# Layer 0's softmax denominators: VectorE adds all four key blocks, TensorE takes two steps a batch in place of four, and all engines get a new order

## The reference

```python
for L in range(4):
    h = relu(layernorm(x))
    x = x + layer[L](h, adj)

# layer 0: 8 heads of 32, q = k = v = LN(h) * gamma1 + beta1
scores = qkv @ qkv.T / sqrt(32);  attn = softmax(where(adj > 0, scores, -inf))
y = h + attn @ qkv;   out = y + gelu(LN(y) @ W1 + b1) @ W2 + b2
# layers 1 and 2: 4 heads of 64, logits = leaky_relu(src_i + dst_j), masked softmax over j, attn @ (h W)
# layer 3: 4 heads of 64, q, k, v projections, masked softmax (diagonal always kept), relu(out @ Wo + bo)
```

## Time and profile before

| | |
|---|---|
| time, median of 3 runs | 4239.26 us (4238.15 to 4240.6) |
| the profiled execution | 4241.92 us, span 4240.1 us |
| TensorE busy | 4042.6 us, 95% |
| VectorE busy | 3223.4 us, 76% |
| ScalarE busy | 2166.5 us, 51% |
| granted TensorE clock, mean | 0.988 |

### The profile page before, as it was taken

The page is one execution under the profiler, slowest core; times in us unless marked ns, Lnnn a source line. Parts: engine busy times, 40 slices in busy tenths (PEclk is TensorE's granted clock), DMA queues, the critical chain, the costliest instruction groups (busy, mean ns, idle before and its releaser), DMA issues.

```text
span 4240.1 us, 58963 instructions
## 1 busy us (share of the span) xinstructions
PE 4042.6 (95%) x22884; PEld 1929.7 (46%) x22884; DVE 3223.4 (76%) x6473; ACT 2166.5 (51%) x3361; POOL 408.3 (10%) x469
## 2 busy tenths in 40 slices
PE   5799999999999999999999999999999999999997
PEld 1344444444444444444444444444444444444443
DVE  5677778877778877777877777877778877788854
ACT  3454555544555554555544555544555544555532
POOL 0001011101011101110100110100110100110100
PEclk9999999999999999999999999999999999999998
DMA  3111111111111111111111111112111111211000
GB/s 99 29 42 50 56 37 49 34 53 51 56 36 51 31 53 52 56 36 51 31 52 54 56 35 51 31 51 56 56 32 54 31 51 56 56 31 46 21 31 31
DMA packets 212311, 193.90 MB, mean 46 GB/s; under 512 B 144448, under 2 KB 179008, under 8 KB 203584
## 3 DMA queue, kind: packets, MB, share of 16 engines
q1 hardware_dynamic: 212032, 190.12, 15.3%
HBM read 138.95 MB, written 17.56 MB: 37 GB/s over the span
## 4 chain that ended last, share of the span: by engine, by line
PE 90%; DVE 5%; ACT 4%; DMA 1%; issue 1%; SPq 0%; POOL 0%; POOLq 0%; ACTq 0%; DVEq 0%
PE O L477 12%; PE M L425 11%; PE M L438 10%; PE S L358 6%; PE S L524 6%; PE O L371 6%; PE M L491 6%; PE O L540 6%; PE M L449 6%; PE O L481 5%; PE M L502 3%; PE M L416 3%; PE M L582 3%; PE O L382 2%; ACT PP L625 2%; PE M L398 2%
## 5 line engine op out<-in xcount | busy, mean ns | idle before, releaser
L1014 DVE SCALAR_TENSOR_TENSOR PG<-g,tcg,mT 128x512 f32<-128x512 f32 x1024 | 691.2, 742 | 33.1 <-PE O L481 21.4
L625 ACT ACTIVATE PP<-S,reach 128x1024 f32<-128x1024 f32 x512 | 542.6, 1111 | 318.8 <-PE O L371 114.5
L906 DVE TENSOR_TENSOR PP<-PP,mT 128x1024 f32<-128x1024 f32 x512 | 597.3, 1218 | 16.5 <-ACT PP L625 16.0
L477 PE MATMUL O<-PG,V 128*32 128x512 f32 x4096 | 550.9, 602 | 18.5 <-DVE PG L1014 17.0
L425 PE MATMUL M<-hT,W 128*128 128x512 f32 x1024 | 460.6, 603 | 3.1 <-ACT hT L660 2.8
L438 PE MATMUL M<-W,H 128*128 128x256 f32 x2048 | 459.7, 378 | 0.0
L438 PEld LDWEIGHTS M<-W,H 128*128 128x128 f32 x2048 | 377.3, 189 | 71.7 <-issue 10.6
L1126 POOL TENSOR_SCALAR ve<-mv 128x4 f32<-128x4 f32 x192 | 97.8, 509 | 3197.4 <-DVE mv L864 3197.4
L358 PE MATMUL S<-hT 32*128 32x512 f32 x2048 | 301.3, 658 | 30.8 <-ACT PP L625 29.4
L739 ACT ACTIVATE PP<-S,sh 128x1024 f32<-128x1024 f32 x256 | 272.1, 1118 | 87.5 <-DVE Q L916 49.0
L603 ACT ACTIVATE V<-z,nb,rs 128x256 f32<-128x256 f32 x128 | 76.6, 602 | 467.4 <-DVE nb L896 467.4
(11 more groups left out here) (136 smaller groups left out, 5608.5 us busy)
## 6 DMA issues: line engine op xcount, KB each, us to landing
g<-t_rows SPq DMA_DIRECT2D x64, 1024.0 KB, 4.7
adj<-adj_in SPq DMA_DIRECT2D x32, 1024.0 KB, 5.5
x<-x_in SPq DMA_DIRECT2D x32, 512.0 KB, 4.0
z<-t_rows SPq DMA_DIRECT2D x64, 256.0 KB, 4.0
out<-x SPq DMA_DIRECT2D x32, 512.0 KB, 2.9
W<-w_in SPq DMA_DIRECT2D x1, 3072.0 KB, 13.0
mT<-z SPq DMA_TRANSPOSE x128, 2.5
m<-V SPq DMA_TRANSPOSE x128, 2.5
```

Of the source, the lines that this page charges most:

```text
L477: e.matmul(k.O[0][r:r + 32, :], s.V[:, jt, 64 * hh + 32 * v:64 * hh + 32 * v + 32], p[:, u, :], start=(jt == 0), stop=(jt == NT - 1))
L625: e.activation(p[:, 2 * pair:2 * pair + 2, :], k.S[:, 2 * pair:2 * pair + 2, :], ACT.Exp, bias=k.reach[:, 7:8], scale=SC0).then_inc(k.e0.s ...
L906: e.tensor_tensor(p[:, 2 * pair:2 * pair + 2, :], p[:, 2 * pair:2 * pair + 2, :], s.mT[:, jt:jt + 1, :].to_broadcast([128, 2, N]), ALU.mul ...
L1014: e.scalar_tensor_tensor(out=p[:, u, :], in0=s.T[hh], scalar=s.tcg[:, 1, hh, jt:jt + 1], in1=s.mT[:, jt, :], op0=ALU.max, op1=ALU.mult).th ...
```

## The change

VectorE now adds all four key blocks of a head group into Q, and TensorE sums Q once for a head group. A new step `pb0` is added, and `pa0` changes: for even i it does what it did; for odd i it adds P[0] to Q, and `pb0(.,i)` adds P[1] to Q. So a batch has twelve adds of 128 x 1024 where it had eight, and two dn0 steps where it had four. The counter `qa`, on which ScalarE waits before it writes P again, is counted by the first add for even i and by pb0 for odd i.

```diff
-    def dn0(self, b, i):
+    def dn0(self, b, q):
         e, k = self.e, self.k
-        if i == 0:
+        if q == 0:
             self.take("O1", k.od0.at(b, 0))
         for h4 in range(4):
-            self.wait_ge(*k.qa.at(b, 2 * i + h4 // 2))
-            m = e.matmul(k.O[1][32 * h4:32 * h4 + 32, :], k.unit[:, i // 2, :], k.Q[:, h4, :],
-                         start=(i == 0), stop=(i == 3))
+            self.wait_ge(*k.qa.at(b, 4 * q + 2 + h4 // 2))
+            m = e.matmul(k.O[1][32 * h4:32 * h4 + 32, :], k.unit[:, q, :], k.Q[:, h4, :], start=(q == 0), stop=(q == 1))
         m.then_inc(k.dn0.sem, 1)
...
     def pa0(self, b, i):
+
         e, k = self.e, self.k
-        self.take("Q", k.dn0.at(b, i))
+        if i % 2 == 0:
+            self.take("Q", k.dn0.at(b, i // 2))
         for pair in range(2):
+            u = slice(2 * pair, 2 * pair + 2)
+            if i % 2 == 0:
+                self.wait_ge(*k.m0.at(b, 4 * i + 2 + pair))
+                e.tensor_tensor(k.Q[:, u, :], k.P[0][:, u, :], k.P[1][:, u, :], ALU.add).then_inc(k.qa.sem, 1)
+            else:
+                self.wait_ge(*k.m0.at(b, 4 * i + pair))
+                self.wait_ge(*k.qa.at(b, 2 * i - 2 + pair))
+                self.mark(e.tensor_tensor(k.Q[:, u, :], k.Q[:, u, :], k.P[0][:, u, :], ALU.add), "half", i // 2, b, pair)
+
+    @step
+    def pb0(self, b, i):
+        e, k = self.e, self.k
+        for pair in range(2):
+            u = slice(2 * pair, 2 * pair + 2)
             self.wait_ge(*k.m0.at(b, 4 * i + 2 + pair))
-            u = slice(2 * pair, 2 * pair + 2)
-            e.tensor_tensor(k.Q[:, u, :], k.P[0][:, u, :], k.P[1][:, u, :], ALU.add).then_inc(k.qa.sem, 1)
+            self.marked("half", i // 2, b, pair)
+            e.tensor_tensor(k.Q[:, u, :], k.Q[:, u, :], k.P[1][:, u, :], ALU.add).then_inc(k.qa.sem, 1)
...
-        do.masks(b0, 0)
...
+        do.pb0(b1, 3)
         do.sh3(b3)
+        do.zb(b1)
```

More of the change, by code:

```diff
@@ L1330, in scalar_program @@
-def scalar_program(do):
[L1332 to L1365, removed]
+        do.b2r(b1, 0, 2)
@@ new lines, in tensor_program @@
+        do.pv3(b3, 1)
+        do.b2r(b1, 0, 3)
+        do.pj(b2, 2, 0)
+        do.pj(b2, 2, 1)
+        do.sc3(b3, 3)
+        do.pj(b2, 2, 2)
+        do.pj(b2, 2, 3)
+        do.dn3(b3, 0)
+        do.pv3(b3, 2)
+        do.prep_b(b1)
+        do.tt(b1, 0, 0)
+        do.tt(b1, 0, 1)
+        do.pv3(b3, 3)
+        do.w1(b1, 0)
+        do.w1(b1, 1)
+        do.dn3(b3, 1)
+        do.grow(b2, 2)
+        do.w1(b1, 2)
+        do.w1(b1, 3)
+        do.w1(b1, 4)
+        do.w1(b1, 5)
+        do.w1(b1, 6)
@@ L1366, in scalar_program @@
+        do.w1(b1, 7)
+        do.w2(b1, 0)
+        do.w2(b1, 1)
+        do.w2(b1, 2)
+        do.w2(b1, 3)
+        do.den3(b3)
+        do.gpv(b2, 2, 0)
+        do.rd3(b3)
+        do.gpv(b2, 2, 1)
+        do.tt(b1, 1, 0)
+def scalar_program(do):
+    for it in range(0, NB + 3):
+        b0, b1, b2, b3 = it, it - 1, it - 2, it - 3
         do.pj(b2, 1, 0)
@@ L1416, in scalar_program @@
         do.sc3(b3, 3)
+        do.pj(b2, 2, 2)
+        do.out3(b3, 0)
+        do.pj(b2, 2, 3)
+        do.ln2(b1, 0)
+        do.ln2(b1, 1)
+        do.ln2(b1, 2)
+        do.ln2(b1, 3)
+        do.tt(b1, 0, 0)
+        do.tt(b1, 0, 1)
+        do.gprep(b2, 2)
+        do.w1(b1, 0)
+        do.w1(b1, 1)
+        do.grow(b2, 2)
+        do.w1(b1, 2)
+        do.w1(b1, 3)
+        do.out3(b3, 1)
+        do.w1(b1, 4)
+        do.w1(b1, 5)
+        do.ln0(b0, 0)
+        do.w1(b1, 6)
+        do.ln0(b0, 1)
+        do.ln0(b0, 2)
+        do.ln0(b0, 3)
+        do.w1(b1, 7)
+        do.lnz(b1, 1, 0)
+        do.lnz(b1, 1, 1)
+        do.rd3(b3)
+        do.lnz(b1, 1, 2)
+        do.lnz(b1, 1, 3)
+        do.tt(b1, 1, 0)
+        do.tt(b1, 1, 1)
 def vector_program(do):
@@ L1422, in vector_program @@
         b0, b1, b2, b3, b4 = it, it - 1, it - 2, it - 3, it - 4
[L1423 to L1476, removed]
         do.pj(b2, 1, 0)
@@ L1581, in gpsimd_program @@
         do.rs(b3, 4)
-        do.rs(b1, 0)
         do.rs(b2, 2)
         do.gmax(b3, 2)
-        do.rs(b1, 1)
+        do.rs(b1, 0)
         do.rs(b2, 3)
 def sync_program(do):
-    for it in range(1, NB + 6):
-        b1, b2, b3, b4, b5, b6 = it - 1, it - 2, it - 3, it - 4, it - 5, it - 6
-        do.store(b6)
-        do.load(b2)
-        do.masks_t(b2, 0)
-        do.masks_t(b2, 1)
-        do.loada(b1)
-        do.trow(b4, 2)
-        do.tbc(b4, 2)
-        do.rrow(b5)
-        do.rbc(b5)
-        do.trow(b3, 1)
-        do.tbc(b3, 1)
+    for it in range(0, NB + 4):
+        b0, b1, b2, b3, b4 = it, it - 1, it - 2, it - 3, it - 4
+        do.masks_t(b1, 1)
+        do.rbc(b4)
+        do.trow(b2, 1)
+        do.loada(b0)
+        do.tbc(b2, 1)
+        do.store(b4)
+        do.load(b0)
+        do.trow(b2, 2)
+        do.masks_t(b0, 0)
+        do.tbc(b2, 2)
+        do.rrow(b3)
     do.end()
```

245 lines of the change are left out of this document (134 added, 111 removed).

## The result

The changed kernel takes 4361.03 us (median; 4360.60 to 4361.85), the kernel before, on the same chip, 4239.93: a ratio of 1.0285, 95% interval 1.0271 to 1.0299. It is slower by 121.1 us. Over 32 batches that is 3.78 us a period; predicted were 4352 us and 3.75 us a period, counted 30 times.

The account below looks back on a forecast made before the run. Bound: a loop of VectorE's part one, then TensorE's part two. 2.35 + 0.9 + 0.5 = 3.75 us a period, times 30 = 112 us on 4239.3: 4352 us; stated range 4231 to 4412, the forecast's own 4302 to 4428.

Parts of the forecast that it names:

- A loop of VectorE's part one and TensorE's part two: Period cut at layer 0's b2r(.,0,2): attention, 62.08 us, set by VectorE; then MLP and projections, 65.55 us, set by TensorE.
- The rival that goes by the highest occupancy: TensorE is the bound all through; 64 dn0 steps go, 63 to 71 us, about 4173 us; chance 0.10.
- VectorE in part one: Layer 0's attention: adds +4.54, zb +1.14, masks -1.22, bst/bag -1.72, TensorE's 0.39 off: +2.35 us (1.7 to 3.2).
- masks: masks(.,0) on VectorE moves out of part one: -1.22 us a period.
- zb: One 128x1024 add on VectorE moved into part one: +1.14 us, also named as cover for ScalarE's late exps.
- TensorE's 0.39: End of part one: TensorE's b2r(.,0,2) starts 0.39 us behind VectorE's normalizing of block 0; taken off VectorE's sum.
- TensorE in part one: Two dn0 steps go, 1.98 to 2.21 us a batch; buys nothing if VectorE sets the end; busy near 58.4.
- TensorE in part two: MLP and projections: waits behind grow 0.44, before tt 0.4, ln2 0.1; in all +0.9 us a period (0.4 to 1.8).
- grow straight ahead of w1(.,2): Part two: with dn3(.,1) no longer between, w1(.,2) waits for the copy that frees M0: +0.44 us a period.
- tt waiting for lnz: Part two: nb(.,3) comes 1.6 us later, lnz follows it, so tt(.,1,0) waits 0.4 us (0 to 0.9).
- rd3 only moves: Part two: moving rd3 on TensorE was charged nothing.
- SyncE: loada between trow(.,1) and tbc(.,1) makes g's rows late; VectorE waits at part one's head: +0.5 us (0 to 1.3).

Follow-up runs that it names:

- The unused adds: Kernel before with four further 128x1024 adds a batch on VectorE, results unused: 4352.55 us with them in part one, 4239.39 us in part two.
- the small dn0: Kernel before with the odd dn0 steps summing 8 columns in place of 512, nothing added on VectorE: 4226.28 us (0.9969).

## Why the prediction was right, step by step

**What bounds the kernel: right.** A loop of VectorE's part one and TensorE's part two. The unused adds (3.63 us a period in part one, 0.0 in part two) and the small dn0 (0.39) show both halves of it, with TensorE's own chain about 1 us behind VectorE in the new order. The rival that goes by the highest occupancy, 4173 us, fell by the same runs: the two dn0 steps are worth 0.39 us a period where it counted on 2.0 to 2.2. In the Trainium skill, "Perfetto Trace Analysis", the rule of the section "Identifying the Most-Contended Engine" (optimize the engine with the highest occupancy first), applied to TensorE's 95%, points the wrong way here. But the same section makes an exception of TensorE, whose headroom it wants judged by MFU and by the busy share of the weight loads: 46% in the earlier trace rows, below VectorE's 76%. What "Perfetto Trace Analysis" in the Trainium skill adds in its section "Optimization Strategy", that the most-contended engine differs between regimes, agrees with the earlier trace rows and these runs.

**VectorE in part one: the sum right, three terms wrong, and by luck they cancelled.** Forecast +2.35, measured 64.35 - 62.08 = +2.27 without the wait for g. But masks gave back 0, not 1.22. Its place in the changed kernel is taken by zb:

```profile
2025.96 2.35 DVE L932 TENSOR_TENSOR Q<-Q,PP 128x1024 f32<-128x1024 f32 x2
...
2028.70 1.22 DVE L968 TENSOR_TENSOR z<-z,W 128x1024 f32<-128x1024 f32 x1
2030.12 2.36 DVE L1060 TENSOR_TENSOR PP<-PP,m 128x1024 f32<-128x1024 f32 x2 [0.19 <-ACT PP L739]
...
2036.22 0.42 DVE L951 TENSOR_TENSOR V<-M,ri 128x256 f32<-128x256 f32 x1
```

zb ends in time for VectorE still to wait 0.19 for the exp, so by this row it costs nothing either (that it is free was not run by itself). The prediction charged zb 1.14 and, a few sentences on, named zb as the cover of the late exp: one piece of work can't be both. The third term is TensorE's 0.39. VectorE is done with block 0 at 2036.64 (the last line), and TensorE starts b2r(.,0,2) at 2036.85, 0.21 later: 0.18 came off, not 0.39. What else came off is VectorE's 0.33 ahead of mx, which is gone in the changed kernel as in the run with the small dn0. By these rows the sum is 4.54 - 1.72 - 0.18 - 0.33 = 2.31. (TensorE's order ahead of the cut is not all as before, as "The change" has it: pv3(.,0) now stands ahead of b2r(.,0,0), and sc3(.,2) between that and b2r(.,0,1).)

**TensorE in part one: right that the time freed on it buys nothing there, wrong that its busy time falls to 58.4.** Measured 60.30. The two dn0 steps left are busy 2.96 us, 1.48 each where four took 1.105 each.

```profile
2027.51 1.91 PE L383 MATMUL O<-Q,unit 128*32 128x512 f32 x8
```

This one takes 1.91, the other 1.04. It runs while pb0's two adds end one after the other (2025.96 to 2028.31). No matmul in it is a long one: one lasts 0.60 us in the mean (598 ns, 603 before). In the step of 1.04 the four heads start within 0.02 us of each other; here the first two start at 2027.51 and the other two at 2028.37, behind the second add. What four heads did side by side two pairs do one after the other. So dn0 falls by 1.46 and not by 2.21. Counted line by line, all of part one falls by 1.3; but the groups of different lines overlap less than before, and so the busy time falls by 0.27 alone (60.57 to 60.30).

**TensorE in part two: forecast +0.9, measured +0.79, from other terms.** grow straight ahead of w1(.,2): forecast 0.44, measured 0.51 by taking it back. tt waiting for lnz: forecast 0.4, measured 0. "rd3 only moves" is the sentence that failed: between the two gpv it costs 0.2 and breaks their run. From den3 to tt it was 2019.40 to 2025.57 = 6.17 before, and in the changed kernel 2081.14 to 2087.66 = 6.52, +0.35, with no idle time ahead of tt (behind tt, where rd3 stood, 0.11 is saved: 2027.39 to 2027.50). den3 before, and the stretch now:

```profile
2019.40 0.95 PE L560 MATMUL M<-e,g 128*128 128x4 f32 x8
```

```profile
2081.14 0.95 PE L560 MATMUL M<-e,g 128*128 128x4 f32 x8
...
2083.76 1.04 PE L481 MATMUL O<-PG,Gp 128*32 128x512 f32 x8
2084.74 0.28 PE L569 MATMUL M<-ident,rd 128*16 128x128 f32 x1
2084.94 1.92 PE L477 MATMUL O<-PG,V 128*32 128x512 f32 x16
...
2087.66 1.09 PE L416 MATMUL M<-ident,z 128*128 128x128 f32 x8
```

What the 0.35 buys the prediction only touched ("can hold VectorE about 1 us"): an early rrow, so that m's transposes are in time.

**SyncE: right.** Forecast 0.5 (0 to 1.3), measured 24.4 / 32 = 0.76 by taking it back. tbc is issued no later than before (1.40 behind trow at 2099.16, 1.41 in the earlier trace rows); what is late is its landing, by 2.2 (6.9 against 4.7).

**The count of periods.** 30 was a little low. The 29 whole periods of the trace take 3812.28 us where they took 3701.60: 110.7, 3.82 each. The two spans differ by 118.7, so the start and the end of the span together cost 8.0, as much as two periods more. With 32 as the count the terms give 2.27 x 32 = 73 us for part one, 0.79 x 32 = 25 for part two and 24 for g, 122 in all where 121 was measured; the 32 is a round figure for the 29 and the two ends.

## What to carry to other kernels

Where two engines take turns, price an edit by the half in which it lies and by which engine ends that half last: the same four adds cost 3.6 us a period or nothing, and two steps of TensorE, at 95% busy, had 0.4 us a period to give. Busy time alone shows neither. A step that stands in a wait which its engine has in any case is free, and gives nothing back when it leaves; so before work is credited or charged, ask what the next instruction would wait for without it, and never use one step both as a cost and as a cover. When a small step moves, follow the DMA that it releases to what queues behind that DMA.

## What was not expected of the hardware

TensorE's busy time rose by 16 us while 512 of its matmul instructions were taken away. A group of matmuls for four heads takes 1.04 us when all four start together, and 1.91 to 2.19 when two of them come late, though one matmul lasts 0.60 us in the mean as before. SyncE's issues keep their order at a price: with adj ahead of tbc the 1 MB of g for layer 1 lands in 6.9 us (median) in place of 4.7. Four transposes take 5.1 us to issue, in the kernel before too (5.13 at 2120.57); put behind a row that comes late they made m late, TensorE idled, and its granted clock fell to 0.50 behind that: the move cost 126 us over the span.
